# A graph attention layer on one core: the weighed values are copied in one piece and brought side by side by DMA

## The chip, the cores and the metric

The kernel runs on one core of one Trainium2 chip. The metric is the device time of one execution in microseconds, lower being better. The median of three runs of the kernel before is 1720.45 us (1720.43 to 1721.51).

## What is computed

One transformer layer over the N = 4096 nodes of a graph, with 128 features, 8 heads of 16 and a hidden width of 512. A query sees only the keys that its row of the 4096 x 4096 integer adjacency matrix marks.

```python
qkv = layer_norm(x, g1, be1) @ w_qkv
q, k, v = ...                                   # (n, 8, 16) each
scores = jnp.einsum('nhd,mhd->hnm', q, k) * SCALE
scores = jnp.where((adj != 0)[None], scores, -jnp.inf)
attn = jax.nn.softmax(scores, axis=-1)
out = jnp.einsum('hnm,mhd->nhd', attn, v).reshape(n, DIM)
x = x + out @ w_proj + b_proj
h2 = layer_norm(x, g2, be2)
ff = jax.nn.gelu(h2 @ w1 + b1) @ w2 + b2
return x + ff
```

## The kernel before

**Tiles and steps.** A short start (LayerNorm 1, keys, values and the first masks) is followed by a loop over 8 tiles of 512 queries and a drain, numbered i = 0 to 8. A tile has 64 steps g: four pairs of heads, 16 steps (QUARTER) for each pair, and in a step two blocks of 128 keys. In the code `b`, `c` and `d` say that a next tile is prepared, that this tile is computed, and that the tile before is being finished; in the drain only `d` holds.

**A step on TensorE.** In this order: row scores for the running maximum of a later pair or tile (`ring_ps`, L1039, two before and two after the scores, taken by VectorE at L817 out of a ring of three banks); masks (L1195) and scores (L1210) of the two blocks into `score_ps`, whose four banks are used two by two in turn; then the weighing of the values with the probabilities of the step that lies LAG = 3 steps back (L1103, `weigh_values`), which sums into the single bank `pv_ps`. ScalarE takes the scores with one exponential for each block (L782, `probs`, 128x1024). In an odd step one of the two blocks gets no mask in PSUM; GpSimd multiplies its probabilities with `keep` (L564, `mask_probs`). So odd and even steps have a slightly different order on TensorE.

**The end of a pair.** The sum of a pair in `pv_ps` has four parts: key block 0 in partitions 0 to 63, key block 1 in 64 to 127, and in each half the two heads of the pair at 32 partitions apiece. Two pairs make a group of four heads (FOURS = 2 groups). At step 3, 19, 35 or 51 of the next pair ScalarE waits for the last weighing (`pv_done`) and brings the two halves side by side into `halves` (`take_values`, L757 and L758), into partitions 0 to 63 for an even pair and 64 to 127 for an odd one. TensorE's first weighing of the new pair waits for that (`values_taken`), since it starts `pv_ps` anew. After an odd pair GpSimd adds the two pieces of `halves` into `attn` (`sum_values`, L627).

**Fills.** Everything else of a tile stands as a "fill" in a numbered step, in a table for ScalarE's banks (`ACT_FILLS`) and one for the ring (`DVE_FILLS`). The engines run their instructions in the order of the code, so a table of step numbers sets the order of TensorE's work. On the ring: "sums" (the softmax sums of four heads, reciprocal on VectorE, L1137 and L917), "back" (these spread over the features and multiplied in, L1144 and L921), "proj" (the projection added to `x_res`, L1152 and L927), "down" (the second feed-forward product, L1161). On ScalarE's banks: "h2t" (the transpose of the rows after LayerNorm 2, L1122 and L735), "up" (steps 21, 23, 25, 27), "q" (33), and "shift" (the maxima moved into the scores, L1006 and L668, steps 5, 13, 29, 31, 37, 45, 53 and 61). A fill in ScalarE's banks at an odd step stands before the weighing of its step, a fill of the ring behind it. LayerNorm 2 has its statistics on VectorE from `LN2_STEP` on and its root and rows on GpSimd at the steps of `POOL_LN2` (L599 to L619).

**DMAs.** Adjacency loads (512 KB), mask transposes and the query copies go through SyncE's queue. ScalarE's queue has three per tile: `x_res` at step 2, `out` at step 35 and `xq` at step 44.

## Time and profile before

| | |
|---|---|
| median of 3 runs | 1720.45 us |
| the profiled execution, as a run | 1722.52 us |
| its span in the profile | 1720.7 us |
| granted TensorE clock, mean | 0.982 |
| busy: TensorE, VectorE, ScalarE, GpSimd | 93%, 82%, 75%, 68% |
| first exponential of tile 0 | 121 us into the span |
| one tile, from the second on | 197.4 us |
| last exponential to the end | 33 us |

The times of the page and of the timelines below are microseconds from the start of the span. A timeline row gives start and duration, engine and line, operation, what it writes and reads, and how many instructions were merged; in brackets stands the idle time of the engine ahead of it and what ended that. PE is TensorE, ACT ScalarE, ACTq ScalarE's queue of DMA issues, DVE VectorE, POOL GpSimd. Tile 3, the fourth, starts at 706 us, and step 51 of it lies near 866 us.

### The profile page before, as it was taken

The numbers are of one execution on the slowest core, as the hardware profiler recorded it, in microseconds if no ns is written. First come the engines' busy times: TensorE is split into PE (matmuls) and PEld (weight loads), VectorE is DVE, ScalarE is ACT, GpSimd is POOL, SyncE is SP. The second block draws the span as 40 slices with busy tenths as digits, with TensorE's granted clock in tenths as the row PEclk, the third lists the DMA queues.
The fourth block names the chain that finished last, engine by engine and source line by source line (L and its number), as shares of the span: only waits on it lengthen the run. The fifth ranks groups of instructions, "written<-read, shape, count | busy, mean of one in ns | idle before, by whom it ended". The sixth has DMA issues, their size and how long they took to land. (4 is left out here: it accounts for less than half of the span.)

```text
span 1720.7 us, 46494 instructions
## 1 busy us (share of the span) xinstructions
PE 1593.7 (93%) x17016; PEld 492.6 (29%) x17016; DVE 1419.5 (82%) x4490; ACT 1297.3 (75%) x1425; POOL 1169.9 (68%) x1092
## 2 busy tenths in 40 slices
PE   6989999999999999999999999999999999999986
PEld 3422222323223232323323232232323232232313
DVE  6888989887998889887899879997898879998701
ACT  4547878788787878778787878778787877878783
POOL 4945487569856798558865789567874698567541
PEclk9879999999999999999999999999999999999998
DMA  7710046202460045400452035500462024500000
GB/s 211 184 50 2 2 134 123 69 2 61 130 129 15 2 117 131 84 2 26 147 109 53 2 97 130 106 2 12 136 127 59 2 63 140 105 2 2 8 1 13
DMA packets 174176, 119.85 MB, mean 70 GB/s; under 512 B 140238, under 2 KB 154447, under 8 KB 173948
## 3 DMA queue, kind: packets, MB, share of 16 engines
q1 hardware_dynamic: 163196, 108.49, 26.1%
q10 hardware_dynamic: 10752, 8.39, 1.7%
q8 instruction: 135, 2.21, 0.5%
q14 instruction: 93, 0.76, 0.1%
HBM read 77.25 MB, written 6.04 MB: 48 GB/s over the span
## 5 line engine op out<-in xcount | busy, mean ns | idle before, releaser
L817 DVE CUSTOM_DVE_ANT_0 masked_out<-ring_ps,row_mask 128x512 bf16<-128x512 f32 x2048 | 1312.6, 688 | 143.5 <-PE ring_ps L1039 102.4
L782 ACT ACTIVATE probs<-score_ps,score_scale 128x1024 f32<-128x1024 f32 x1024 | 1089.0, 1112 | 334.7 <-PE score_ps L1210 326.7
L564 POOL TENSOR_TENSOR probs<-probs,keep 128x1024 int32<-128x1024 int32 x256 | 605.0, 2364 | 281.4 <-ACT probs L782 269.9
L1103 PE MATMUL pv_ps<-probs,v_ones 128*17 128x512 f32 x4096 | 543.6, 598 | 4.4 <-POOL probs L564 3.3
L1039 PE MATMUL ring_ps<-k_stack,q_stack 51*64 51x512 f16 x4096 | 485.7, 397 | 15.1 <-DVE row_max L817 14.4
L1210 PE MATMUL score_ps<-q_stack,k_stack 51*64 51x512 f16 x4096 | 374.0, 391 | 19.7 <-ACT probs L782 0.3
L1195 PE MATMUL score_ps<-mask_t,ident_bf 64*64 64x512 bf16 x3072 | 281.3, 388 | 49.6 <-ACT probs L782 31.6
L1039 PEld LDWEIGHTS ring_ps<-k_stack,q_stack 51*64 51x64 f16 x4096 | 164.9, 104 | 493.1 <-DVE row_max L817 443.4
L1210 PEld LDWEIGHTS score_ps<-q_stack,k_stack 51*64 51x64 f16 x4096 | 117.3, 104 | 217.6 <-PE score_ps L1195 185.9
L817 DVE DVE_READ_ACCUMULATOR2_ANT row_max<- 128x1 f32 x2048 | 170.4, 83 | 0.0
L1195 PEld LDWEIGHTS score_ps<-mask_t,ident_bf 64*64 64x64 bf16 x3072 | 91.5, 105 | 211.2 <-ACT probs L782 163.0
L503 POOL TENSOR_SCALAR row_mask<-row_mask 128x1024 bf16<-128x1024 bf16 x124 | 129.9, 1047 | 23.6 <-POOL row_mask L499 23.2
L499 POOL TENSOR_SCALAR row_mask<-adj_in 128x1024 bf16<-128x1024 uint32 x124 | 129.3, 1042 | 4.2 <-DVE row_max L817 2.1
L1103 PEld LDWEIGHTS pv_ps<-probs,v_ones 128*17 128x17 f32 x4096 | 72.9, 95 | 145.7 <-issue 87.7
L508 POOL TENSOR_SCALAR max_unit<-neg_max 128x4 f32<-128x4 f32 x64 | 12.7, 199 | 78.7 <-DVE neg_max L827 78.1
L917 DVE RECIPROCAL recip<-ring_ps 128x16 f32<-128x16 f32 x16 | 4.1, 258 | 70.4 <-PE ring_ps L1137 70.4
L668 ACT COPY q_stack<-score_ps 2x256 f16<-2x256 f16 x128 | 46.7, 365 | 9.2 <-PE score_ps L1006 6.9
L556 POOL TENSOR_SCALAR keep<-mask_t 128x512 int32<-128x512 bf16 x64 | 39.8, 622 | 5.4
L934 DVE TENSOR_TENSOR rows<-ring_ps,x_res 128x128 f32<-128x128 f32 x32 | 9.3, 292 | 40.0 <-PE ring_ps L1161 40.0
L701 ACT ACTIVATE hidden<-score_ps,part_coef 128x512 f16<-128x512 f32 x36 | 28.0, 778 | 15.3 <-PE score_ps L1064 12.4
L1127 PE MATMUL score_ps<-h2T,w_sb 128*128 128x512 f32 x64 | 36.9, 666 | 1.9 <-ACT h2T L735 1.0
L1161 PEld LDWEIGHTS ring_ps<-w_sb,hidden 128*128 128x128 f32 x256 | 30.7, 191 | 25.5 <-DVE row_max L817 23.8
(121 smaller groups left out, 811.7 us busy)
## 6 DMA issues: line engine op xcount, KB each, us to landing
adj_in<-adj SPq DMA_DIRECT2D x128, 512.0 KB, 4.2
q_stack<-q_dram SPq DMA_DIRECT2D x42, 64.0 KB
mask_t<-row_mask SPq DMA_TRANSPOSE x128, 3.4
xq<-xnT_dram ACTq DMA_DIRECT2D x8, 256.0 KB, 2.6
x_res<-x ACTq DMA_DIRECT2D x8, 256.0 KB, 4.5
out<-rows ACTq DMA_DIRECT2D x8, 256.0 KB, 2.5
xnT_dram<-attn ACTq DMA_DIRECT2D x4, 256.0 KB, 3.7
xnT_dram<-halves ACTq DMA_DIRECT2D x4, 256.0 KB, 2.1
```

What stands on the lines that cost most here:

```text
L499: nc.gpsimd.tensor_scalar(target, adj_in[:, half, :].bitcast(U32), 1.0, 0.0, ALU.min, ALU.max)\
L503: nc.gpsimd.tensor_scalar(target, target, BIG, -BIG, ALU.mult, ALU.add).then_inc(mask_done, 1)
L556: nc.gpsimd.tensor_scalar(keep[:, KEPT.index(m), :], mask_t[:, m, :], 1.0 / BIG, 1.0, ALU.mult, ALU.add)\
L564: nc.gpsimd.tensor_tensor(view, view, keep[:, KEPT.index(m), :].unsqueeze(1).broadcast_to([128, 2, TILE]), ALU.mult).then_inc(probs_masked, 1)
L668: last = nc.scalar.copy(stack[r:r + SHIFT_PARTS, p, 256 * jj:256 * (jj + 1)], bank.bitcast(F16)[r:r + SHIFT_PARTS, 0:256])
L782: nc.scalar.activation(probs[:, (2 * g + n) % SLOTS, :], score_ps[:, half:half + 2, :].rearrange("p a n -> p (a n)"), ACT.Exp, scale=score ...
L817: nc.vector.tensor_tensor_reduce(out=masked_out[:, place % 3, :], in0=ring_ps[:, place % 3, :], in1=row_mask[:, j, ch * 512:(ch + 1) * 512 ...
L1039: last = nc.tensor.matmul(ring_ps[64 * t:64 * (t + 1), place % 3, :], stack[rows, p, first:first + 64], k_stack[rows, p, ch, K_FIRST:], st ...
L1103: last = nc.tensor.matmul(pv_ps[32 * k:32 * k + HD + 1, :], v_ones[:, block_of(g, b), 2 * p + a, :], probs[:, (2 * g + b) % SLOTS, a * TIL ...
L1127: last = nc.tensor.matmul(bank, w1_sb[:, 128 * f:128 * (f + 1)], h2T[:, :], start=True, stop=True)
L1195: last = nc.tensor.matmul(bank[to, :], ident_bf[keys, keys], mask_t[keys, source, :], start=True, stop=False)
L1210: last = nc.tensor.matmul(bank[64 * t:64 * (t + 1), :], k_stack[rows, p, m // 4, at + 64 * t:at + 64 * (t + 1)], q_stack[par][rows, p, :], ...
```

## The change

`take_values` copies all 128 partitions of `pv_ps` at once. For an even pair the target is `halves[:, 0, :]`, for an odd pair the group's own plane of `attn`. A new function `move_values` issues DMAs on ScalarE's queue behind the first exponential of that step (in the drain, right behind the copy): for an even pair one of 64 partitions by 512, inside `halves`; for an odd pair, once the even pair's DMA has landed, two of that size out of `attn` into `halves`. Each is 128 KB. GpSimd's addition waits for the three landings (`values_moved`) in place of the copies, and stands one step later. So do the sums, back, projection and LayerNorm 2 steps on all engines; h2T moves from step 17 to step 19.

```diff
-H2T_STEP = 17
+H2T_STEP = 19
...
-DVE_FILLS = {4: ("sums", FOURS - 1), 5: ("back", FOURS - 1, 0, 2), 6: ("back", FOURS - 1, 2, 4),
-             7: ("proj", 0), 8: ("proj", 1)}
+DVE_FILLS = {5: ("sums", FOURS - 1), 6: ("back", FOURS - 1, 0, 2), 7: ("back", FOURS - 1, 2, 4),
+             8: ("proj", 0), 9: ("proj", 1)}
...
-DVE_FILLS.update({2 * QUARTER + 4: ("sums", 0), 2 * QUARTER + 5: ("back", 0, 0, SUB)})
+DVE_FILLS.update({2 * QUARTER + 5: ("sums", 0), 2 * QUARTER + 6: ("back", 0, 0, SUB)})
...
-PROJ_STEP = 7
-LN2_STEP = 8
-POOL_LN2 = [12, 13, 14, 15, 16, 18]
+BACK_STEP = 6
+PROJ_STEP = 8
+LN2_STEP = 9
+POOL_LN2 = [13, 14, 15, 16, 17, 19]
...
             def sum_values(n, f):
 
-                pool.wait_ge(values_taken, n)
+                pool.wait_ge(values_moved, (n // 2) * (16 * 3))
...
-                    if d and g == LAG + 1:
+                    if d and g == LAG + 2:
                         sum_values(i * PAIRS, FOURS - 1)
-                    if c and g == 2 * QUARTER + LAG + 1:
+                    if c and g == 2 * QUARTER + LAG + 2:
                         sum_values(i * PAIRS + 2, 0)
...
             def take_values(n, p, seen):
 
                 act.wait_ge(pv_done, seen)
                 if n >= 2:
                     act.wait_ge(attn_ready, n // 2)
-                own = slice(64 * (p % 2), 64 * (p % 2 + 1))
-                nc.scalar.copy(halves[own, 0, :], pv_ps[0:64, :])
-                nc.scalar.copy(halves[own, 1, :], pv_ps[64:128, :]).then_inc(values_taken, 1)
+                nc.scalar.copy(halves[:, 0, :] if p % 2 == 0 else attn[:, p // 2, :], pv_ps[:, :]).then_inc(values_taken, 1)
+
+            def move_values(n, p):
+
+                act.wait_ge(values_taken, n + 1)
+                if p % 2 == 0:
+                    act.dma_start(halves[0:64, 1, :], halves[64:128, 0, :]).then_inc(values_moved, 16)
+                else:
+                    act.wait_ge(values_moved, (n // 2) * (16 * 3) + 16)
+                    act.dma_start(halves[64:128, 0, :], attn[64:128, p // 2, :]).then_inc(values_moved, 16)
+                    act.dma_start(halves[64:128, 1, :], attn[0:64, p // 2, :]).then_inc(values_moved, 16)
...
                     if d and g == LAG:
                         take_values(i * PAIRS - 1, PAIRS - 1, i * STEPS)
+                        if not c:
+                            move_values(i * PAIRS - 1, PAIRS - 1)
...
+                            if n == 0 and g % QUARTER == LAG and (g > QUARTER or d):
+
+                                move_values(i * PAIRS + (g // QUARTER - 1), (g // QUARTER - 1) % PAIRS)
```

ScalarE in tile 1, from step 14 to the first exponentials of step 22; L735 (before) and L736 (now) take h2T, L744 and L745 (now L745 and L746) the first "up". Before:

```order
L782 ACTIVATE probs<-score_ps,score_scale 128x1024 x8
L735 ACTIVATE h2T<-score_ps,gb 128x512
L782 ACTIVATE probs<-score_ps,score_scale 128x1024 x2
L757 COPY halves<-pv_ps 64x512
L758 COPY halves<-pv_ps 64x512
L782 ACTIVATE probs<-score_ps,score_scale 128x1024 x6
L744 ACTIVATE hidden<-score_ps,b_col 128x512
L745 ACTIVATE q_x<-score_ps,b_col 128x512
```

And now, where L794 is the exponential and L758 the one copy:

```order
L794 ACTIVATE probs<-score_ps,score_scale 128x1024 x10
L758 COPY halves<-pv_ps 128x512
L794 ACTIVATE probs<-score_ps,score_scale 128x1024
L764 DMA halves<-halves 64x512
L794 ACTIVATE probs<-score_ps,score_scale 128x1024
L736 ACTIVATE h2T<-score_ps,gb 128x512
L794 ACTIVATE probs<-score_ps,score_scale 128x1024 x4
L745 ACTIVATE hidden<-score_ps,b_col 128x512
L746 ACTIVATE q_x<-score_ps,b_col 128x512
```

h2T has moved behind the copy and both exponentials of step 19, and a DMA stands between these.

GpSimd in the same tile, steps 35 to 38: L499 and L503 turn adjacency into a mask, L564 masks probabilities, L627 adds the halves. Before:

```order
L503 TENSOR_SCALAR row_mask<-row_mask 128x1024
L627 TENSOR_TENSOR attn<-halves 128x512
L564 TENSOR_TENSOR probs<-probs,keep 128x1024
L499 TENSOR_SCALAR row_mask<-adj_in 128x1024
L503 TENSOR_SCALAR row_mask<-row_mask 128x1024
L564 TENSOR_TENSOR probs<-probs,keep 128x1024
```

And now (the lines are numbered one higher):

```order
L504 TENSOR_SCALAR row_mask<-row_mask 128x1024
L565 TENSOR_TENSOR probs<-probs,keep 128x1024
L628 TENSOR_TENSOR attn<-halves 128x512
L500 TENSOR_SCALAR row_mask<-adj_in 128x1024
L504 TENSOR_SCALAR row_mask<-row_mask 128x1024
L565 TENSOR_TENSOR probs<-probs,keep 128x1024
```

The addition stands behind the masking of step 35 now, and ahead of a conversion.

TensorE in tile 1, from the weighing of step 4 to the first "back". Before:

```order
L1103 MATMUL pv_ps<-probs,v_ones 17x512 x4
L1137 MATMUL ring_ps<-sum_sel,attn 128x4 x4
L1039 MATMUL ring_ps<-k_stack,q_stack 64x512 x4
L1210 MATMUL score_ps<-q_stack,k_stack 64x512 x4
L1195 MATMUL score_ps<-mask_t,ident_bf 64x512 x4
L1210 MATMUL score_ps<-q_stack,k_stack 64x512 x4
L1039 MATMUL ring_ps<-k_stack,q_stack 64x512 x4
L1006 MATMUL score_ps<-ident_h,max_part 2x128 x4
L1103 MATMUL pv_ps<-probs,v_ones 17x512 x4
L1144 MATMUL ring_ps<-ident,recip 32x128 x8
```

And now:

```order
L1118 MATMUL pv_ps<-probs,v_ones 17x512 x4
L1054 MATMUL ring_ps<-k_stack,q_stack 64x512 x4
L1225 MATMUL score_ps<-q_stack,k_stack 64x512 x4
L1210 MATMUL score_ps<-mask_t,ident_bf 64x512 x4
L1225 MATMUL score_ps<-q_stack,k_stack 64x512 x4
L1054 MATMUL ring_ps<-k_stack,q_stack 64x512 x4
L1021 MATMUL score_ps<-ident_h,max_part 2x128 x4
L1118 MATMUL pv_ps<-probs,v_ones 17x512 x4
L1152 MATMUL ring_ps<-sum_sel,attn 128x4 x4
```

The sums have gone from step 4 to behind the weighing of step 5, where "back" stood.

## Rows read from the trace of the kernel before

**Rows 1.** The page, part 1: busy time of each engine.

```profile
PE 1593.7 (93%) x17016; PEld 492.6 (29%) x17016; DVE 1419.5 (82%) x4490; ACT 1297.3 (75%) x1425; POOL 1169.9 (68%) x1092
```

**Rows 2.** Timeline of ScalarE, tile 3, steps 50 and 51.

```profile
863.94 2.12 ACT L782 ACTIVATE probs<-score_ps,score_scale 128x1024 f32<-128x1024 f32 x2 [1.16 <-PE score_ps L1210]
865.95 0.57 ACT L757 COPY halves<-pv_ps 64x512 f32<-64x512 f32 x1
866.53 0.58 ACT L758 COPY halves<-pv_ps 64x512 f32<-64x512 f32 x1
867.14 2.12 ACT L782 ACTIVATE probs<-score_ps,score_scale 128x1024 f32<-128x1024 f32 x2
```

**Rows 3.** Timeline of TensorE, weighings of steps 48, 49, 50, masks and weighing of 52.

```profile
858.90 1.05 PE L1103 MATMUL pv_ps<-probs,v_ones 128*17 128x512 f32 x8
...
861.70 1.05 PE L1103 MATMUL pv_ps<-probs,v_ones 128*17 128x512 f32 x8
...
864.36 1.05 PE L1103 MATMUL pv_ps<-probs,v_ones 128*17 128x512 f32 x8
...
869.32 0.41 PE L1195 MATMUL score_ps<-mask_t,ident_bf 64*64 64x512 bf16 x4 [0.44 <-ACT probs L782]
...
870.35 1.05 PE L1103 MATMUL pv_ps<-probs,v_ones 128*17 128x512 f32 x8
```

**Rows 4.** Line 731: duration in ns, least, median and most.

```profile
L731 ACT COPY q_x<-score_ps x7: 592/592/592, 222.8 to 1406.2; 128x512 f32<-128x512 f32 x7
```

**Rows 5.** Timelines of TensorE and ScalarE, tile 4, steps 2 to 4.

```profile
909.46 1.05 PE L1103 MATMUL pv_ps<-probs,v_ones 128*17 128x512 f32 x8
...
912.38 2.12 ACT L782 ACTIVATE probs<-score_ps,score_scale 128x1024 f32<-128x1024 f32 x2
...
914.55 0.41 PE L1195 MATMUL score_ps<-mask_t,ident_bf 64*64 64x512 bf16 x4 [0.44 <-ACT probs L782]
...
915.59 1.05 PE L1103 MATMUL pv_ps<-probs,v_ones 128*17 128x512 f32 x8
```

**Rows 6.** Timelines of TensorE and ScalarE, tile 3, steps 17 and 19.

```profile
759.49 0.63 PE L1122 MATMUL score_ps<-ident,rows 128*128 128x128 f32 x4 [0.18 <-POOL rows L613]
...
764.27 0.57 ACT L757 COPY halves<-pv_ps 64x512 f32<-64x512 f32 x1
...
765.16 0.45 PE L1039 MATMUL ring_ps<-k_stack,q_stack 51*64 51x512 f16 x4
```

**Rows 7.** Timelines of TensorE and ScalarE, tile 3, step 35.

```profile
819.25 0.39 PE L1210 MATMUL score_ps<-q_stack,k_stack 51*64 51x512 f16 x4
...
819.83 1.11 ACT L782 ACTIVATE probs<-score_ps,score_scale 128x1024 f32<-128x1024 f32 x1
```

**Rows 8.** Timeline of TensorE, tile 4: weighings of steps 5, 6, 7, first "back".

```profile
919.48 0.62 PE L1103 MATMUL pv_ps<-probs,v_ones 128*17 128x512 f32 x2
...
920.35 0.69 PE L1144 MATMUL ring_ps<-ident,recip 128*32 128x128 f32 x16
...
922.66 1.05 PE L1103 MATMUL pv_ps<-probs,v_ones 128*17 128x512 f32 x8
...
925.76 1.05 PE L1103 MATMUL pv_ps<-probs,v_ones 128*17 128x512 f32 x8
```

**Rows 9.** Timeline of ScalarE and its queue, tile 3, steps 42 to 44.

```profile
841.69 4.29 ACT L782 ACTIVATE probs<-score_ps,score_scale 128x1024 f32<-128x1024 f32 x4 [1.15 <-PE score_ps L1210]
844.88 0.34 ACTq L770 DMA_DIRECT2D xq<-xnT_dram  x1
```

**Rows 10.** The page, part 6: DMA issues, KB each, median us to landing.

```profile
x_res<-x ACTq DMA_DIRECT2D x8, 256.0 KB, 4.5
out<-rows ACTq DMA_DIRECT2D x8, 256.0 KB, 2.5
```

**Rows 11.** Timeline of all engines, the drain: second copy and GpSimd's addition.

```profile
1690.48 0.58 ACT L758 COPY halves<-pv_ps 64x512 f32<-64x512 f32 x1
1691.24 1.26 POOL L627 TENSOR_TENSOR attn<-halves 128x512 f32<-128x512 f32 x1 [2.52 <-ACT halves L758]
```

## What the change was predicted to do

> **What bounds the kernel now.** I read the page's busy times first. TensorE is busy for 93% of the span, VectorE 82%, ScalarE 75%, GpSimd 68% [rows 1]. That says only that TensorE is near the end of every step. What a shorter ScalarE copy is worth has to be read where the copies stand, so the next view is the timeline of ScalarE and of TensorE around one of them.
>
> Step 51 of the fourth tile is the plain case. The marker of a step is the start of its weighing matmuls (L1103). Steps 48, 49 and 50 start them at 858.90, 861.70 and 864.36, so two steps take 5.46 us: 2.80 for the first (an odd step's start follows an even one's) and 2.66 for the second [rows 3]. Step 52 starts them at 870.35, which is 5.99 us after step 50: 0.53 us more than a plain pair. The cause is in the same two timelines. ScalarE ends its exponentials of step 50 at 866.06 and then makes the two copies of 64 partitions, 0.57 and 0.58 us [rows 2]; step 51's first exponential starts at 867.14, the second ends at 869.26. TensorE's second set of masks of step 52 needs the PSUM banks that this exponential reads, and starts at 869.32 after an idle 0.44 us charged to `probs` [rows 3]. So at this place the path runs through ScalarE: copy, copy, exponential, exponential, masks. Elsewhere TensorE and VectorE hold each other and ScalarE has its 1.16 us of idle time in every pair of steps [rows 2].
>
> There are 32 places with the copies: steps 19, 35 and 51 of 8 tiles, step 3 of 7, and the drain behind the last tile. All tiles between the first and the last repeat to a few hundredths, so one tile is enough for each kind of place.
>
> **Part 1: one copy in place of two.** A copy of 128 partitions by 512 from PSUM takes 0.592 us (`q_x`, seven times) [rows 4], against 0.575 + 0.583 for the two [rows 2]: 0.58 us less on ScalarE, 32 times. The number of partitions costs nothing here.
> - Step 51: the second exponential would end at 868.68, and the masks of step 52, 0.06 behind it, could start at 868.74 in place of 869.32. The pair is 0.53 us over a plain one, which is all that can be won, give or take a few hundredths; I take 0.55 us. Eight tiles: 4.4 us.
> - Step 3: the exponential starts at 912.38 right behind the copies, and again the second masks start late, at 914.55 after 0.44 us of idle time; steps 2 to 4 take 909.46 to 915.59 = 6.13 us, 0.67 over a plain pair [rows 5]. Taking 0.58 away leaves 0.1 of that. Seven tiles: 4.1 us.
> - Step 19 in the first tile, which has no fill for h2T: it has the same shape as step 51, 0.5 us once.
> - Step 35: here a "down" fill has made TensorE late. Step 35's first scores start at 819.25 and are complete near 819.7; the exponential starts at 819.83, behind the copies, so only 0.1 us is at stake and the next pair is not longer [rows 7]. I take 0, and 0.3 us once in the first tile, which has no such fill.
>
> Together 4.4 + 4.1 + 0.5 + 0.3 = 9.3 us.
>
> **Part 2: h2T at step 19 in place of 17.** The fill goes to the step that has the copy. At step 17 its transposes start at 759.49 and take TensorE 0.63 us, after an idle 0.18 us [rows 6]. They need the bank that the step's first exponential reads. At step 19 TensorE issues its row scores at 765.16, about 0.45 us long; with one copy from 764.27 [rows 6] the first exponential runs from 764.88 to 765.99, so the transposes can start only near 766.1 and the weighing near 766.7, 1.1 later than now. The next step then runs without the old wait of 0.44 us, so about 0.65 is left, which is what step 17 gives back. So in the seven tiles with the fill step 19 gains 0 (from +0.5 to -0.5 each).
>
> **Part 3: the sums, back, projection and LayerNorm fills one step later.** Their work stays; the parity of the step changes. The second "back" fill, behind even step 6, makes the next interval 925.76 - 922.66 = 3.10, or 0.30 over 2.80; the first, behind odd step 5, 922.66 - 919.48 = 3.18, or 0.52 over 2.66 [rows 8]. A fill behind an even step is thus about 0.2 cheaper, since an odd step has a mask wait that absorbs it. Before, three of the five stood behind even steps (4, 6, 8), now two (6, 8); steps 36 and 37 swap one for one. I take +0.15 (the sums are not a whole "back") in 7 tiles, 1.0 us; the range is 0 to 2, or -2 if parting sums from the shift fill of step 5 helps.
>
> **Part 4: 48 DMAs on ScalarE's queue and their waits.** A DMA issue takes ScalarE's sequencer 0.34 us beside a running exponential: the one of `xq` at 844.88 lies inside a run of four exponentials without a gap [rows 9]. For an odd pair, two issues and a wait on the copy's own semaphore, 0.8 us in all, stand between the first and the second exponential of the step. The first runs for 1.11 us, so 0.3 us is over. Cost 0; if that cover is missing, up to 0.3 us for 15 odd pairs, 4 us.
>
> Behind them stands GpSimd, whose addition now waits for the landings, with its masking of step 5 or 37 queued behind it; behind that stands TensorE's sums fill. At step 3 the second DMA would be issued near 912.2 to 912.6. The slot in which TensorE wants the sums is where "back" stands now, 920.35 [rows 8], less 1.0 for the sums that have left step 4 and less the 0.6 gained: 918.8. The addition takes 1.26 us [rows 11] and 0.15 to be seen, so the landing may take about 4.8 us. No row shows an SBUF to SBUF copy. Nearest are DMAs on the same queue, of twice the size: `out`, issued in step 35 itself, 2.5 us, and `x_res`, issued at step 2, 4.5 us [rows 10]. I take 3 us, nearer to `out`, because the data are half as much: hidden, with 1.8 us to spare. At step 35 the slot is 827.5 by the same working, and more is left.
>
> The drain hides nothing. There the second copy ends at 1691.06 and the addition starts at 1691.24 [rows 11]. Now the copy ends 0.58 earlier, two issues follow (0.4 us until the second), and a landing of 2.0 to 3.0 us, around the 2.5 of `out` [rows 10]: I take 2.4, since the data are half as much. Net +0.4 + 2.4 - 0.6 = +2.2 us, from 1.8 to 2.8.
>
> The Trainium skill (SBUF — State Buffer, section "The DMA setup-cost knee") speaks against this edit: each transfer pays about 2 us that no size reduces. Its port table gives 64 partitions 218 GB/s, and the section on two DMAs says that they serialize. By the page, an estimate, 128 KB takes 2.6 us and two of them 3.2, so the drain would lose 3.0 instead of 2.2 and the sum be 0.8 us higher. No run so far shows such a pair.
>
> **Sum.** -9.3 + 0 + 1.0 + 0 + 2.2 = -6.1 us. The profiled span goes from 1720.7 to 1714.6 and its run's time from 1722.5 to 1716.4. The profiled run stood 2.1 us over the median of the runs; I carry the difference over, so the median goes from 1720.45 to 1714.3.
>
> **Rivals.**
> - The gain goes at step 19. If h2T's transposes and its pass on ScalarE meet the copy worse than I worked out, 0.5 us is lost in each of seven tiles, and step 3 keeps its remaining wait; 3.5 us go back: 1717.8, within 0.2% of before. For it: at step 19 TensorE waits on ScalarE alone, with no slack. Against: the next step absorbs. Chance 0.20. A missing cover for the issues (part 4) gives the same time, and so does a path that VectorE takes over once ScalarE is early.
> - More gain. Parting the sums from the shift fill saves 0.3 to 0.5 per tile, step 35 gives 0.1: 1711. Chance 0.15.
> - Late landings, the case on the other side. The place is the sums fill of steps 5 and 37: TensorE takes its work in order, so its row scores stand still until GpSimd has added. The point from which it decides: a landing over 4.8 us at step 3 and 5.9 at step 35. At 6.5 us, step 3 loses 1.7 in 7 tiles and step 35 0.6 in 8, 16.7 us: 1731. All of the gain is gone from 5.7 us on. For it: `x_res` needs 4.5 us in the median at step 2. Against: `out` needs 2.5 with step 35's loads beside it. Chance 0.12.
> - The copy is not one piece in cost (128 partitions slower from `pv_ps`), or the masks wait is not cut: between 1719 and 1722.5. The row of `q_x` speaks against it [rows 4]. Chance 0.05.
>
> **Chances.** Forecast 0.48, at 1714.3, from 1711.5 to 1717.5 by the bounds of parts 2 and 3 and the drain. Something over 0.2% (3.4 us) is what a measurement of this kernel can tell from no change. Faster by more: the forecast, the larger gain and a quarter of the first rival, 0.67. Within: 0.19. Slower: 0.14, the late landings and part of the last case. The range 1708.5 to 1721.5 leaves out the late landings and little else.
>
> **What would show it.** Right: one copy of 0.59 us per pair; at step 51 the two-step interval falls from 5.99 to about 5.4 to 5.5, and at step 3 from 6.13 to about 5.55; no idle time of TensorE before the sums fill outside the drain; landings under 4.8 us; GpSimd's addition in the drain 2 to 3 us later after the last weighing. Wrong: step 19's pair at over 6.6 us; exponentials with a gap between the first and the second of steps 3 and 35; TensorE idle before the sums with GpSimd's addition named.

## The result

The changed kernel takes 1715.28 us in the median of 9 runs (1713.18 to 1717.54), the kernel before in the same rounds 1721.51 (1717.41 to 1722.56). The ratio is 0.9965, with a 95% interval of 0.9954 to 0.9975: 0.35% or about 6 us faster. Forecast were 1714.3 us and a gain of 6.1.

The profiled execution of the changed kernel has a span of 1711.4 us, 9.3 less than the 1720.7 of before, so it flatters the change by some 3 us. The page, parts 1 and 6 (issues, KB each, median us from issue to landing), answers to [rows 1, 10]:

```profile
PE 1592.9 (93%) x17016; PEld 496.3 (29%) x17016; DVE 1418.5 (83%) x4490; ACT 1275.2 (75%) x1393; POOL 1167.7 (68%) x1092
...
halves<-attn ACTq DMA_DIRECT2D x32, 128.0 KB, 2.6
...
halves<-halves ACTq DMA_DIRECT2D x16, 128.0 KB, 2.2
x_res<-x ACTq DMA_DIRECT2D x8, 256.0 KB, 4.6
out<-rows ACTq DMA_DIRECT2D x8, 256.0 KB, 5.5
```

ScalarE is busy for 22 us less (32 instructions fewer), and the span shows less than half of that. The copies themselves are 18.3 us of it (64 of 0.57 to 0.59 us before, 32 of 0.58 to 0.59 now); nearly all of the rest is that the instruction behind the copy now overlaps it, as step 51 shows below. I split the span at the start of the first exponential and at that of the last one:

| us | before | changed | difference |
|---|---|---|---|
| start, up to the first exponential | 121.35 | 118.56 | -2.8 |
| loop, first to last exponential | 1564.85 | 1555.54 | -9.3 |
| drain, last exponential to the end | 34.5 | 37.3 | +2.8 |

The start is the same code in both. What differs is the granted TensorE clock between 60 and 100 us. That stretch of the kernel before (busy times of TensorE, its weight loads, VectorE, ScalarE and GpSimd, then the clock, the DMA share and GB/s):

```profile
60.00:100.00 40.00, 38.12 (x194) 17.29 (x194) 32.09 (x99) 25.14 (x43) 37.20 (x49) 0.87 0.69 165
```

and of the changed kernel:

```profile
60.00:100.00 40.00, 36.97 (x206) 15.98 (x205) 36.00 (x111) 27.04 (x46) 38.38 (x50) 1.00 0.68 164
```

The changed kernel's execution had the full 2.4 GHz there, that of before had the 1.2 GHz level for a part. It is luck of one execution: over the twelve profiles of this study, the first exponential starts anywhere from 116.8 to 121.5 us. In the loop, tile 4 of the changed kernel takes 198.7 us, 2.3 more than the 196.4 of the same tile in e10 and e12 (two of the experiments below), with one long DMA issue and one stretch at the lower clock in it. The median of nine runs is the better measure, and it says 6 us.

**Step 51**, tile 3, the changed kernel, weighings of steps 50, 51 and 52 on TensorE (L1118 is L1103 of before), against [rows 3]:

```profile
856.38 1.05 PE L1118 MATMUL pv_ps<-probs,v_ones 128*17 128x512 f32 x8
859.24 1.05 PE L1118 MATMUL pv_ps<-probs,v_ones 128*17 128x512 f32 x8
861.90 1.05 PE L1118 MATMUL pv_ps<-probs,v_ones 128*17 128x512 f32 x8
```

The pair of steps takes 5.52 us in place of 5.99; the idle 0.44 us charged to `probs` is gone. ScalarE at the same place, against [rows 2]:

```profile
855.97 2.12 ACT L794 ACTIVATE probs<-score_ps,score_scale 128x1024 f32<-128x1024 f32 x2 [1.16 <-PE score_ps L1225]
857.98 0.58 ACT L758 COPY halves<-pv_ps 128x512 f32<-128x512 f32 x1
858.45 1.14 ACT L794 ACTIVATE probs<-score_ps,score_scale 128x1024 f32<-128x1024 f32 x1
858.60 0.47 ACTq L764 DMA_DIRECT2D halves<-halves  x1
859.45 1.13 ACT L794 ACTIVATE probs<-score_ps,score_scale 128x1024 f32<-128x1024 f32 x1
```

One copy of 0.58 us, and the DMA issue inside the first exponential; the second follows 1.00 us behind the first, as without a DMA. The exponential starts 0.47 us behind the start of the copy. Before, 1.19 us lay between the start of the first copy and the exponential (865.95 and 867.14 in [rows 2]), so ScalarE comes 0.72 us earlier and not only the 0.58 of one copy. The rest is overlap: this exponential starts 0.11 us before the copy's record ends, where the one of before started 0.02 us behind the second copy's end.

**Step 3**, tile 3: the odd pair, with two issues.

```profile
706.10 0.59 ACT L758 COPY attn<-pv_ps 128x512 f32<-128x512 f32 x1
706.56 1.14 ACT L794 ACTIVATE probs<-score_ps,score_scale 128x1024 f32<-128x1024 f32 x1
706.71 0.47 ACTq L767 DMA_DIRECT2D halves<-attn  x1
707.22 0.62 ACTq L768 DMA_DIRECT2D halves<-attn  x1
707.94 1.11 ACT L794 ACTIVATE probs<-score_ps,score_scale 128x1024 f32<-128x1024 f32 x1 [0.24 <-issue]
```

Before, ScalarE's records at an odd pair did not overlap at all: in tile 4 the exponentials of step 2 end at 911.16, the first copy follows, and the next exponential starts at 912.38 [rows 5].

```profile
911.18 0.58 ACT L757 COPY halves<-pv_ps 64x512 f32<-64x512 f32 x1
```

Now the exponential starts 0.46 us behind the start of the copy, but the cover for the issues is too short. The issues take 0.47 and 0.62 us, and ScalarE stands idle for 0.24 us between the two exponentials. TensorE feels it at the second set of masks of step 4, with the weighings of steps 2 and 4 around it (of before: [rows 5]):

```profile
704.51 1.05 PE L1118 MATMUL pv_ps<-probs,v_ones 128*17 128x512 f32 x8
...
709.11 0.41 PE L1210 MATMUL score_ps<-mask_t,ident_bf 64*64 64x512 bf16 x4 [0.16 <-ACT probs L794]
710.15 1.05 PE L1118 MATMUL pv_ps<-probs,v_ones 128*17 128x512 f32 x8
```

The pair of steps takes 5.64 us, in place of 6.13. The landings come in time: GpSimd adds at 710.61, TensorE wants the sums at 714.14, with more than 2 us between the end of the one and the start of the other.

```profile
710.61 1.28 POOL L628 TENSOR_TENSOR attn<-halves 128x512 f32<-128x512 f32 x1
...
714.14 1.06 PE L1152 MATMUL ring_ps<-sum_sel,attn 128*128 128x4 f32 x8
```

**The drain**, against [rows 11]: copy, two issues, GpSimd's addition, and TensorE's wait for it, which was 2.82 us before.

```profile
1677.77 0.58 ACT L758 COPY attn<-pv_ps 128x512 f32<-128x512 f32 x1 [2.55 <-PE pv_ps L1118]
1678.38 0.47 ACTq L767 DMA_DIRECT2D halves<-attn  x1
1678.88 0.62 ACTq L768 DMA_DIRECT2D halves<-attn  x1
...
1681.47 1.26 POOL L628 TENSOR_TENSOR attn<-halves 128x512 f32<-128x512 f32 x1 [4.88 <-DMA halves<-attn]
...
1682.88 1.84 PE L1152 MATMUL ring_ps<-sum_sel,attn 128*128 128x4 f32 x8 [5.18 <-POOL attn L628]
```

From the start of the copy to that of the addition it takes 3.70 us. Before, from the start of the first copy, it was 1691.24 - 1689.89 = 1.35 us. That is 2.35 us more.

### The profile page after: what moved, and what is told of

It reads as the page before. It is cut to its first block, busy times and chain, and to the rows that moved or that the text cites. A ratio compares the mean times of both kernels' runs of the same rounds, so it can differ in the third digit from the quotient of the medians.

```text
span 1711.4 us, 46526 instructions
## 1 busy us (share of the span) xinstructions
PE 1592.9 (93%) x17016; PEld 496.3 (29%) x17016; DVE 1418.5 (83%) x4490; ACT 1275.2 (75%) x1393; POOL 1167.7 (68%) x1092
## 4 chain that ended last, share of the span: by engine, by line
PE 53%; ACT 22%; issue 14%; POOL 8%; DVE 2%; ACTq 1%; DMA 0%; POOLq 0%; DVEq 0%
ACT probs L794 20%; PE pv_ps L1118 15%; PE ring_ps L1054 10%; PE score_ps L1210 10%; PE score_ps L1225 9%; POOL probs L565 2%; PE ring_ps L1176 2%; PE score_ps L1142 2%; POOL k_stack L526 2%; ACT q_stack L669 1%; DVE masked_out L832 1%; PE ring_ps L1167 1%; PE ring_ps L1152 1%; PE ring_ps L1159 1%; POOL hidden L588 1%
## 5 line engine op out<-in xcount | busy, mean ns | idle before, releaser
L794 ACT ACTIVATE probs<-score_ps,score_scale 128x1024 f32<-128x1024 f32 x1024 | 1089.9, 1112 | 346.9 <-PE score_ps L1225 334.3
L1118 PE MATMUL pv_ps<-probs,v_ones 128*17 128x512 f32 x4096 | 544.6, 600 | 3.2 <-POOL probs L565 3.2
L1054 PEld LDWEIGHTS ring_ps<-k_stack,q_stack 51*64 51x64 f16 x4096 | 169.3, 104 | 496.3 <-DVE row_max L832 448.5
L1210 PEld LDWEIGHTS score_ps<-mask_t,ident_bf 64*64 64x64 bf16 x3072 | 93.0, 105 | 195.6 <-ACT probs L794 150.2
L1118 PEld LDWEIGHTS pv_ps<-probs,v_ones 128*17 128x17 f32 x4096 | 72.4, 95 | 139.9 <-issue 72.9
L574 POOL TENSOR_SCALAR q_x<-q_x 128x512 f32<-128x512 f32 x14 | 8.7, 621 | 45.1 <-ACT q_x L746 45.1
```

The costliest lines, as they stand in the source:

```text
L794: nc.scalar.activation(probs[:, (2 * g + n) % SLOTS, :], score_ps[:, half:half + 2, :].rearrange("p a n -> p (a n)"), ACT.Exp, scale=score ...
L1054: last = nc.tensor.matmul(ring_ps[64 * t:64 * (t + 1), place % 3, :], stack[rows, p, first:first + 64], k_stack[rows, p, ch, K_FIRST:], st ...
L1118: last = nc.tensor.matmul(pv_ps[32 * k:32 * k + HD + 1, :], v_ones[:, block_of(g, b), 2 * p + a, :], probs[:, (2 * g + b) % SLOTS, a * TIL ...
L1210: last = nc.tensor.matmul(bank[to, :], ident_bf[keys, keys], mask_t[keys, source, :], start=True, stop=False)
```

## The experiments

All times of steps below are worked out from the starts of the weighing matmuls. For each of the 64 intervals I take the median of tiles 1 to 6; most agree to a few hundredths where the clock is full. A column sums the medians of the steps named, the last one all 64. So it leaves out what only single tiles have, and is a little shorter than a whole tile (197.0 against 197.4 us before).

| us per tile | steps 2 to 4 (copy) | 4 to 16 (sums to LayerNorm 2) | 16 to 18 (h2T before) | 18 to 21 (copy, h2T now) | 50 to 55 (copy) | tile |
|---|---|---|---|---|---|---|
| before | 6.13 | 38.33 | 6.15 | 9.94 | 14.77 | 197.0 |
| changed | 5.64 | 38.38 | 5.45 | 10.44 | 14.13 | 195.7 |
| e1, steps only | 6.12 | 38.38 | 5.45 | 11.14 | 14.76 | 197.5 |
| e2, one copy only | 5.50 | 38.32 | 6.15 | 9.45 | 14.13 | 195.2 |
| e3, h2T at 17 | 5.66 | 38.38 | 6.54 | 9.45 | 14.14 | 195.8 |
| e6, no DMAs | 5.50 | 38.36 | 5.45 | 10.44 | 14.13 | 195.6 |
| e7, DMAs before the exponential | 6.65 | 38.38 | 5.45 | 11.15 | 14.76 | 198.3 |
| e10, second DMA later | 5.50 | 38.36 | 5.45 | 10.44 | 14.13 | 195.6 |
| e13, h2T in time | 5.50 | 38.45 | 6.15 | 9.44 | 14.13 | 195.3 |

My theory: the gain is 0.58 us of ScalarE at steps 3, 19 and 51; the moved steps give nothing by themselves; DMAs cost the drain 2 to 3 us and the loop little. Rivals: the gain comes from the moves; the gain needs them; the drain's loss is the clock.

**e1, the step numbers alone.**

```diff
-H2T_STEP = 17
+H2T_STEP = 19
...
-PROJ_STEP = 7
-LN2_STEP = 8
-POOL_LN2 = [12, 13, 14, 15, 16, 18]
+PROJ_STEP = 8
+LN2_STEP = 9
+POOL_LN2 = [13, 14, 15, 16, 17, 19]
```

(and the two `DVE_FILLS` rows and GpSimd's steps of the change; two copies, no DMAs)

> The kernel before with the step numbers of the change alone (h2T at 19, sums to LayerNorm 2 one step later), still two copies and no DMAs. My theory (the gain is the copy's length on ScalarE at steps 3, 19 and 51, the moves give nothing by themselves): the waits of 0.44 us ahead of the masks at steps 4 and 52 stay, and h2T behind two copies costs step 19 about 0.5 us more; 0.3 to 0.6 us more per tile, 2 to 4 us slower than before. Rival (parting the sums from the shift fill of step 5 is where the gain comes from): 0.5 to 1 us less per tile, 4 to 8 us faster than before.

1725.16 us, ratio 1.0029 (1.0019 to 1.0040): 4.9 us slower. The moves are a cost. In the table it stands in one column: h2T in the step of two copies takes 11.14 us for steps 18 to 21 in place of 9.94, and gives only 0.70 back at step 17. Its transposes wait for the exponential behind the two copies, here in tile 3:

```profile
764.78 0.66 PE L1123 MATMUL score_ps<-ident,rows 128*128 128x128 f32 x4 [1.04 <-ACT probs L783]
```

In the changed kernel, with one copy, that wait is 0.34 us. The rival that parting the sums from the shift fill brings the gain is out: steps 4 to 16 are the same to 0.05 us.

**e2, one copy alone.**

```diff
-                own = slice(64 * (p % 2), 64 * (p % 2 + 1))
-                nc.scalar.copy(halves[own, 0, :], pv_ps[0:64, :])
-                nc.scalar.copy(halves[own, 1, :], pv_ps[64:128, :]).then_inc(values_taken, 1)
+                nc.scalar.copy(halves[:, 0, :], pv_ps[:, :]).then_inc(values_taken, 1)
```

> The kernel before with one copy of 128 partitions in place of the two, everything else as before; the second half is not brought beside the first, so GpSimd adds what is not the sum (part of the computation left out). My theory: step 51's pair falls from 5.99 to about 5.45 us, step 3's from 6.13 to about 5.6, step 19's from 5.95 to about 5.45; 1.5 to 1.7 us per tile and 0.6 in the drain, 11 to 14 us faster than before, more than the change itself, since neither DMAs nor h2T at step 19 take of it. Rival (the gain needs the moved steps): under 4 us.

This kernel leaves out a part of the computation: the halves are not brought side by side, and GpSimd adds what does not belong together. 1707.23 us, ratio 0.9921 (0.9895 to 0.9947): 13.6 us faster. Its weighings of steps 50, 51 and 52:

```profile
856.06 1.05 PE L1101 MATMUL pv_ps<-probs,v_ones 128*17 128x512 f32 x8
858.91 1.05 PE L1101 MATMUL pv_ps<-probs,v_ones 128*17 128x512 f32 x8
861.57 1.05 PE L1101 MATMUL pv_ps<-probs,v_ones 128*17 128x512 f32 x8
```

5.51 us, as in the changed kernel, with all fills at their old steps. The one copy is the gain, 1.8 us per tile. The change keeps 1.3 of it per tile, and less than half of the 13.6 us in all.

**e3, h2T back at step 17.**

```diff
-H2T_STEP = 19
+H2T_STEP = 17
...
-POOL_LN2 = [13, 14, 15, 16, 17, 19]
+POOL_LN2 = [12, 13, 14, 15, 16, 18]
```

> The changed kernel with h2T back at step 17 and GpSimd's LayerNorm 2 steps as before, so that it is not in the step of the copy. If h2T at step 19 eats the gain of that step: 0.2 to 0.3 us less per tile than the changed kernel, 1.5 to 2 us less in all; step 19's pair about 5.45 us. Rival (GpSimd comes too late for step 17, since VectorE's statistics still stand one step later): TensorE waits for GpSimd's rows at step 17, no gain or up to 1 us per tile slower.

1712.81 us, ratio 0.9959 (0.9945 to 0.9974), its interval overlapping that of the changed kernel. The rival mechanism holds: steps 18 to 21 win the 0.99 us, and step 17 loses 1.09. Line 1137 (h2T's transposes) of this kernel, the idle time ahead of them by what ended it:

```profile
L1137 PE MATMUL score_ps<-ident,rows x32: 272/273/448, 358.2 to 1694.8; 128*128 128x128 f32 x32
...
  POOL rows L614: 3.5, 7
```

GpSimd's rows are 0.5 us late in each of the seven tiles, as the statistics stand one step later. So in the change h2T had to move because the sums had moved.

**e4, the drain by copies.** In the drain alone, where ScalarE has nothing else to do:

```diff
+            def take_last(n, seen):
+
+                act.wait_ge(pv_done, seen)
+                act.wait_ge(attn_ready, n // 2)
+                act.wait_ge(values_moved, (n // 2) * (16 * 3) + 16)
+                nc.scalar.copy(halves[64:128, 0, :], pv_ps[0:64, :])
+                nc.scalar.copy(halves[64:128, 1, :], pv_ps[64:128, :]).then_inc(values_taken, 1)
```

> The changed kernel, but in the drain ScalarE copies the two halves side by side as before, without a DMA, and GpSimd waits for the copies. If the DMAs cost the drain 2.6 us (from 5.04 to 7.62 us between the start of the last exponential and the addition): 2.6 us less than the changed kernel, nothing else moved. Rival (the drain's 3.0 us are TensorE's lower clock): under 1 us less.

1711.91 us, ratio 0.9954 (0.9936 to 0.9971), against 0.9965 of the changed kernel: 1.9 us by the ratios, with intervals that overlap. The 7.62 us of the expectation are 7.37 in the trace of the changed kernel (1674.10 to 1681.47), so 2.3 us were to be won. The trace is plainer than the runs. GpSimd's addition starts 1.35 us behind the start of the first copy again, not 3.70:

```profile
1677.85 0.58 ACT L760 COPY halves<-pv_ps 64x512 f32<-64x512 f32 x1 [2.57 <-PE pv_ps L1129]
1678.44 0.58 ACT L761 COPY halves<-pv_ps 64x512 f32<-64x512 f32 x1
1679.20 1.26 POOL L631 TENSOR_TENSOR attn<-halves 128x512 f32<-128x512 f32 x1 [2.52 <-ACT halves L761]
```

Behind the addition all drains have the same code, and from its start to the end they still take 29.0 to 31.6 us over the twelve profiles, with the lower clock at different places in them. So the whole drain (34.5 us before, 37.3 changed, 35.6 here) measures this less well than the rows.

**e5, the DMAs with the steps of before.** The changed kernel with all step numbers of `DVE_FILLS`, `LN2_STEP`, `POOL_LN2`, `H2T_STEP` and GpSimd's addition put back.

> The changed kernel with all step numbers as before (sums at steps 4 and 36, h2T at 17). The copies and DMAs are those of the change. The sums' slot on TensorE comes about one step earlier, near 4.9 us after the copy of step 3 and 4.8 after that of step 35; the second landing (2.6 us, 4.4 in the profile's worst case, issued 0.6 us behind the copy) and the addition of 1.27 us end after 4.5 to 6.3 us. If landings decide: TensorE idles ahead of the sums with the addition named, 0.5 to 2 us per tile, and eats the 0.5 us per tile that h2T at 17 gives (tile length 195.5 to 197.5 us). Rival (landings are early enough for step 4 too, so that the later steps were not needed): tile length near the 195.2 us of the kernel with one copy alone, 2 to 4 us faster than the changed kernel.

1727.96 us (1721.78 to 1736.13), ratio 1.0043 (1.0025 to 1.0061): slower than before the change. This is the rival of the late landings, made real by a deadline one step earlier. TensorE's sums, line 1152, wait for GpSimd's addition in nine of sixteen places. One is the drain with its 5.18 us, which the changed kernel has too; the other eight, 8.7 us together, lie in the loop:

```profile
L1152 PE MATMUL ring_ps<-sum_sel,attn x128: 244/253/356, 229.8 to 1703.7; 128*128 128x4 f32 x128
...
  POOL attn L628: 13.9, 9
```

The typical tile is only 0.6 us longer than the changed kernel's, at 196.3 us. More than the waits costs what follows them. Tile 1, TensorE, and then three stretches of it (the clock as above):

```profile
321.10 1.05 PE L1118 MATMUL pv_ps<-probs,v_ones 128*17 128x512 f32 x8
324.16 1.41 PE L1152 MATMUL ring_ps<-sum_sel,attn 128*128 128x4 f32 x8 [2.01 <-POOL attn L628]
```

```profile
322.00:324.50 2.50, 0.49 (x8) 0.37 (x4) 0.67 (x4) 0.92 (x1) 1.66 (x2) 1.00 0.00 1
325.00:331.80 6.80, 6.72 (x63) 2.84 (x63) 3.33 (x11) 2.96 (x4) 5.85 (x4) 0.52 0.01 2
332.00:336.00 4.00, 3.92 (x64) 1.50 (x60) 3.85 (x12) 3.02 (x3) 0.00 (x0) 1.00 0.00 0
```

TensorE idled for 2.01 us, the granted clock then went from 2.4 to 1.2 GHz for 6.8 us, and the tile took 204.8 us, 8.5 more than the typical one, with one more such stretch in it. In this execution there are six of them between the start and the drain, in that of the changed kernel one, in that of before none. Each of the six begins within about 3 us of a wait of 0.49 to 2.01 us for the addition; a wait of 0.69 us at 527 had none behind it. The loop of this execution (1734.27 us, one of the slowest of the ten) is 18.6 us longer than the changed kernel's, although h2T at step 17 gives 0.3 us per tile back and the 2.3 us of tile 4 are absent. So by my estimate some 14 us stand beside the 8.7 us of waits.

**e6, no DMAs.** `move_values` is not called, and GpSimd waits for `values_taken`.

> The changed kernel without its 48 DMAs; GpSimd waits for the copies (the halves are not brought side by side, part of the computation left out). Issues on ScalarE's queue took 0.47 us for the first and 0.62 to 1.38 for the second, and at step 3 the second exponential started 1.01 us late. If that costs: step 3's pair falls from 5.64 to 5.50 us as in the kernel with one copy alone, 1 us in all in the loop, and the drain loses its 2.6 us: 3 to 4 us less than the changed kernel. Rival (the DMAs slow the loop in more places, by traffic): over 5 us less. Rival (they are free in the loop): 2.6 us less, all in the drain.

Here too the halves are not brought side by side, so a part of the computation is left out. 1709.01 us, ratio 0.9937 (0.9922 to 0.9952), so 4.8 us less than the changed kernel by the ratios. Of the loop it takes 0.14 us per tile, at step 3 alone (5.50 in place of 5.64), 1 us in all; the addition in the drain comes 2.9 us sooner after the last exponential. The loop shows no traffic cost of the 6.3 MB. The 1.01 us of the expectation was tile 4 alone; in the other tiles the second exponential came 0.24 us late. Against e2, which differs by the moved steps alone, e6 is 2.8 us slower by the ratios, with intervals that overlap, and 0.35 us per tile in the table. So by the ratios, of the 13.6 us the moved steps took back 2.8 and the DMAs 4.8, most of it in the drain.

**e7, the DMAs ahead of the first exponential.** `move_values` is called right behind `take_values`.

> The changed kernel with the DMAs issued right behind the copy, ahead of the step's first exponential. Then the wait for the copy's own semaphore (about 0.07 us) and the issues (0.47 us for an even pair, 0.47 + 0.62 or more for an odd one) stand on ScalarE's path: 0.5 us more at step 51, 1.1 to 1.9 at step 3, some 0.5 at step 19, little at step 35; 2 to 3 us per tile, 14 to 22 us more than the changed kernel. Rival (issues run beside whatever ScalarE does, so their place is of no account): under 3 us more.

1735.87 us, ratio 1.0082 (1.0062 to 1.0103), 20 us more than the changed kernel and 2.6 per tile. The cover is what makes the DMAs cheap. Step 3, tile 3:

```profile
716.32 0.58 ACT L758 COPY attn<-pv_ps 128x512 f32<-128x512 f32 x1
716.93 0.47 ACTq L767 DMA_DIRECT2D halves<-attn  x1
717.44 0.61 ACTq L768 DMA_DIRECT2D halves<-attn  x1
718.15 2.12 ACT L794 ACTIVATE probs<-score_ps,score_scale 128x1024 f32<-128x1024 f32 x2 [1.25 <-PE score_ps L1222]
```

The exponential follows the copy by 1.25 us, which the view puts down to the scores; it is the queue that held it.

**e10, the second DMA one exponential later.**

```diff
+                            if n == 1 and g % (2 * QUARTER) == LAG and (g > QUARTER or d):
+                                move_second((g // QUARTER - 1) % PAIRS)
```

> The changed kernel with the second DMA of an odd pair issued behind the second exponential of the step. Only one issue stands between the two exponentials: if the pair of issues opened the gap of 1.01 us at step 3, step 3's pair falls from 5.64 to 5.50 us, 1 us less in all, and the landing, 1.1 us later, is still in time. Rival (the second landing then comes too late): TensorE idles ahead of the sums of step 5, over 1 us more per tile.

1712.95 us, ratio 0.9959 (0.9944 to 0.9973). That is 1.0 us less than the changed kernel by the ratios, with intervals that overlap, so the rows show it and the runs do not. Step 3's pair is 5.50 us, the same as without DMAs, and ScalarE's idle time between the exponentials is gone (the second one at 906.36 follows the first by 1.00):

```profile
905.36 1.14 ACT L798 ACTIVATE probs<-score_ps,score_scale 128x1024 f32<-128x1024 f32 x1
905.51 0.48 ACTq L771 DMA_DIRECT2D halves<-attn  x1
906.11 0.57 ACTq L762 DMA_DIRECT2D halves<-attn  x1
906.36 1.14 ACT L798 ACTIVATE probs<-score_ps,score_scale 128x1024 f32<-128x1024 f32 x1
```

**e12, e10 and e4 together.**

> The changed kernel with the second DMA of an odd pair behind the second exponential, and the drain by copies without DMAs. If the two effects add: tile length 195.55 us and a drain 2.1 us or more shorter, 3 to 4 us less than the changed kernel, about 10 us faster than before. Rival (the drain's gain was run to run variation of the clock): 1 to 1.5 us less only.

1708.18 us, ratio 0.9929 (0.9916 to 0.9943): 12.2 us faster than before, and its interval lies below that of the changed kernel. The ratios say 6.2 us less than the change, where I expected 3 to 4; the two edits by themselves gave 1.9 and 1.0. The traces show less of it as the edits': the loop is 2.7 us shorter (1552.8 against 1555.5), of which 0.8 is the 0.12 to 0.17 of each of five tiles and 2.3 is tile 4 with its stretch at the lower clock (the first tile gives 0.3 back), and the addition in the drain comes 2.35 us sooner. Whether stretches like that of tile 4 are rarer in e12 was not measured apart.

**e13, h2T in time.** The whole back fill of the tile in step 6, so that projection and LayerNorm 2 keep their steps of before with the sums in step 5.

```diff
-DVE_FILLS = {5: ("sums", FOURS - 1), 6: ("back", FOURS - 1, 0, 2), 7: ("back", FOURS - 1, 2, 4),
-             8: ("proj", 0), 9: ("proj", 1)}
+DVE_FILLS = {5: ("sums", FOURS - 1), 6: ("back", FOURS - 1, 0, SUB), 7: ("proj", 0), 8: ("proj", 1)}
```

(`H2T_STEP`, `PROJ_STEP`, `LN2_STEP` and `POOL_LN2` as before the change; the other back fill is parted in two)

> The kernel e12 with the whole of the tile's back fill in step 6, so that projection and LayerNorm 2 keep their old steps (7 and 8, 8 to 11) although the sums stand in step 5; h2T and GpSimd's LayerNorm 2 steps as before the change. If h2T at 17 failed to gain only because GpSimd's rows came 0.5 us late (3.5 us of idle time of TensorE ahead of seven transposes): steps 16 to 18 take 6.15 us in place of 6.54 and the tile 195.2 to 195.4 us, 1 to 2.5 us less in all than e12. Rival (a whole back fill in one step stalls TensorE and VectorE more than two halves): no gain or slower.

1707.73 us, ratio 0.9925 (0.9913 to 0.9937), not to be told from e12 by the runs. Its loop is 3.5 us shorter than that of e12 in the trace (1549.3 against 1552.8 us), and steps 16 to 18 take 6.15 us, so the explanation of e3 holds. Of the 3.5 us, h2T's return is 2.0 (steps 16 to 21: 15.60 in place of 15.89). Another 1.1 is not its doing but that of the other back fill, now in two halves (steps 35 to 40: 15.51 in place of 15.65). The drain of this execution had 1.2 GHz for 20 us and gave 2.3 of that back.

## Why the prediction was right

**What bounds it (right).** The two copies stood on the path at steps 3 and 51, through the second exponential and the masks, and nowhere near it at step 35. Measured in the loop, changed against before:

| term | forecast | measured |
|---|---|---|
| step 51, 8 tiles | -4.4 | -5.1 (0.64 each) |
| step 3, 7 tiles | -4.1 | -3.4 (0.49 each) |
| h2T and step 19, 7 tiles | 0 | -1.4 (0.20 each) |
| sums to LayerNorm 2, 7 tiles | +1.0 | +0.3 |
| steps 35 to 40 | 0 | 0 |
| first tile beyond step 51 | -0.8 | -1.1 |
| drain, up to the addition | +2.2 | +2.3 |

The first tile's row is its 1.77 us less 0.64. The terms sum to -8.4; the forecast was -6.1, and the runs say -6.2, with an interval from -7.9 to -4.3. So four terms were mis-sized by 0.7 to 1.4 us and cancel only in part, and that forecast and runs agree to 0.1 us is luck. In the profiled execution 2.3 us of tile 4 stand against the sum; what does so in the other runs is not known. The mechanism is shown by e2 (the copy alone gives 13.6 us) and e1 (the moves alone lose 4.9).

**Part 1, ScalarE's gain (mis-sized).** I took one copy less, 0.58 us. The rows give ScalarE 0.72 us at step 51, since the exponential now overlaps the copy. At step 3 it is 0.87 us, since there the copy now also overlaps the exponential ahead of it (from the exponentials of step 2 to that of step 3 it took 3.34 us and takes 2.47). So step 51 gained 0.64 us on the path, not 0.55: 0.48 until step 52 and the rest in the steps up to 55, so the 0.53 over a plain pair was not all that could be won. At step 3 I wrote that 0.58 of the 0.67 would go. The copy gives 0.63 in e2 and e6, as far as a plain pair lets it. But 0.14 is taken back, which leads to the step that was wrong.

**Part 4, the cover of the DMA issues (wrong).** I took 0.34 us an issue from `xq` and found 0.3 us left under the exponential. The issues of these DMAs take 0.47 and 0.62 us, 1.1 together, so the cover was missing in every odd pair: 0.24 us of idle time on ScalarE at step 3 and 0.19 at step 35, and 0.14 us on the path at step 3. The gap between the two exponentials was one of my signs of being wrong, and it came. The bound I gave for that case, up to 0.3 us for each odd pair, held in size. At step 35 it costs nothing (steps 35 to 40 take 15.65 us as before). Once, at 903.57 in tile 4, the second issue took 1.38 us; that opened a gap of 1.01 us, and cost the tile 0.8 us. Why it took so long stays open.

```profile
903.57 1.38 ACTq L768 DMA_DIRECT2D halves<-attn  x1
905.05 1.11 ACT L794 ACTIVATE probs<-score_ps,score_scale 128x1024 f32<-128x1024 f32 x1 [1.01 <-PE pv_ps L1118]
```

**Part 4, landings (right).** I took 3 us and had 4.8 to spend. The median is 2.6 us for an odd pair's DMAs and 2.2 for an even pair's single one, the longest 4.4, and TensorE never waits for the sums in the loop.

In the drain the first of the two landed 2.3 us after its issue and the second, issued 0.50 us later, 2.4 after its own. So both were down 2.9 us after the first issue. The Trainium skill (SBUF — State Buffer, the DMA setup-cost knee and the port table), with its fixed 2 us and half the port rate, made an estimate of 2.6 us for one and 3.2 for two. Both are 0.3 to 0.4 us above what was measured, and whether the two take turns these landings do not tell. The +3.0 us that I drew from it for the drain also counted the 3.2 us from the second issue; from the first it is 3.2 - 0.6 = +2.6, against 2.35 measured and my 2.2 from the rows.

**Part 2, h2T at step 19 (right that it eats the gain, by 0.2 us too pessimistic).** Steps 16 to 21 take 15.89 us in place of 16.09: I had +0.65 at step 19 and -0.65 at step 17, and measured are +0.50 and -0.70. What step 19 could give is 0.49 (e2), and h2T's move eats 0.3 of it. I had not seen why h2T was moved at all. Rows of GpSimd that come late is the answer of e3, and the row of the trace that says it had been in front of me: the transposes already waited 0.18 us for them at step 17 [rows 6], in two of the seven tiles.

**Part 3, parity of the steps (small).** The later sums cost 0.05 us per tile, not 0.15. That a fill behind an even step is cheaper holds: half a "back" adds 0.31 us behind step 6, and 0.44 to 0.50 behind steps 7 and 5. Parting the sums from the shift fill, the rival's reason for more gain, gave nothing: they add 0.95 us to the interval that holds the shift and 1.05 to the one that does not.

**The rival of the late landings (right as a mechanism).** It did not happen here, because the sums stand one step later. e5 shows that with the steps of before it does, with landings like those measured, and turns 6 us of gain into 7 us of loss. The price I gave counted only the waits. The clock that follows them was left out, and in the profiled execution of e5 it is, by the estimate there, the larger part.

## What to carry to other kernels

Before a copy is made shorter, read which engine the next wait names: here the same edit was worth 0.64 us at one step and nothing at another, and all of it sat on an engine that is 75% busy. Read also whether its neighbours overlap it: that made 0.72 us out of 0.58. A copy between partitions by DMA is cheap where the issue lies under a running instruction and the reader comes 4 us or more later; it costs its full landing where nothing covers it, so the drain of a loop deserves its own version. When a fill is moved for one deadline, follow those behind it: the later sums pushed LayerNorm 2, that pushed h2T onto the step of the copy, and the two together gave back a fifth of what the copy had won (0.35 of 1.8 us per tile).

## What was new about the hardware

- On ScalarE, the instruction behind a copy of 64 partitions by 512 from PSUM started 0.02 us after the copy's end, all 63 times in the trace of before. Behind a copy of 128 partitions, where nothing else held it, the exponential started 0.12 us before the end, 23 times in the trace of the change. What decides that was not tried.
- A DMA of 64 partitions by 2 KB between SBUF regions took ScalarE's queue 0.47 to 0.51 us to issue, the second in a row 0.61 to 0.63 us (once 1.38). Stores and loads of 128 partitions by 2 KB between SBUF and DRAM (`xnT_dram`, `xq`) took 0.32 to 0.36 us.
- An `out` store issued right behind the pair of them took 0.51 us to issue and landed after 5.5 us, against 0.38 and 2.5 before (medians). Nothing waits for it until step 50.
- The granted clock fell from 2.4 to 1.2 GHz within a microsecond of TensorE's 2.01 us of idle time in e5. Behind the 1.04 to 1.05 us of idle time ahead of h2T's transposes at step 19 it fell in one of seven tiles in e1, and in three of seven in e7. In the changed kernel it fell at 937.7 us in tile 4, 33 us after the late exponential, with TensorE busy for 2.5 of the 3.4 us before. An idle time of 0.70 us stands there in e4 and e10 too, without a fall, so its cause was not found. Stretches ahead, during and behind:

```profile
934.00:937.40 3.40, 2.50 (x28) 0.62 (x20) 3.33 (x12) 2.36 (x4) 1.88 (x6) 1.00 0.02 5
937.40:940.90 3.50, 3.35 (x28) 0.73 (x28) 1.90 (x7) 1.83 (x4) 2.82 (x4) 0.54 0.00 0
940.90:944.00 3.10, 2.81 (x36) 0.64 (x28) 2.77 (x11) 2.57 (x3) 1.71 (x7) 0.97 0.00 0
```
